# Attention: queries and keys are turned once, transfers gather each group's rows, and only the row maxima are turned in the loop

## The chip, the core and the metric

The kernel runs on one core of one Trainium2 chip. Its time is the device time of one execution in microseconds (us). The engines are TensorE (PE, with its weight loads as PEld), VectorE (DVE), ScalarE (ACT), GpSimd (POOL) and SyncE (SP), which here only issues DMAs. SBUF is the on-chip memory of 128 partitions, PSUM holds the matmul results in banks of 512 float32 per partition.

## The reference

Six layers run one after the other on 1024 tokens of width 256. The second, an attention, is what the change is about; the fifth, a state-space mixer, is touched in one place. Everything is float32.

```python
x = x + 0.5 * moe(layernorm(x))            # 8 experts, top 2
x = x + attention(layernorm(x))            # this change
x = x + 0.5 * moe(layernorm(x))
x = x + 0.5 * sparse_ffn(layernorm(x))
x = x + mamba(layernorm(x))                # one edit in its preparation
x = x + 0.5 * sparse_ffn(layernorm(x))

# attention: 32 query heads and 8 key heads of width 8
q, k = rope(x @ Wq.T), rope(x @ Wk.T);  v = x @ Wv.T
scores = einsum('bkgqd,bkld->bkgql', q, k) * 8 ** -0.5
out = einsum('bkgql,bkld->bkgqd', softmax(scores), v)
return out @ Wo.T
```

## The kernel before

The attention works through 8 groups, one per key head, with 4 query heads each. Scores are computed twice. **Chunks** (`score_chunk`, L1087) have queries on the partitions: one matmul makes 128 queries x 512 keys of one head, and VectorE takes the row maximum of each (`reduce`, L863). A group has 64 chunks, 32 for each half of its queries. Then **scoresT** (L1103) makes the same scores with keys on the partitions, this time less the row maximum, ScalarE takes the exponential (L981), and `values` (L1115) multiplies by the values; the values carry a column of ones, so that a row of the result is the softmax sum. The row maximum enters scoresT as two more rows of the contraction (a high and a low part of the maximum against two rows of -1), just as queries and keys enter in high and low parts to keep float32 accuracy.

The loop of a group has 16 **slots**: 8 key tiles for each half of the queries. In each slot TensorE runs, in an order that is written out in `body`: scoresT of heads pair 0, two chunks, scoresT of pair 1, a chunk, `values` of the slot before, a chunk. The chunks run `LEAD = HALF + 2 * PER_SLOT` = 32 + 8 = 40 chunks ahead of the exponentials, and from slot 6 on they belong to the next group. They go round three PSUM banks (`ring`): a table decides at build time which bank a job gets, and `take` makes TensorE wait until the bank's last reader is done.

Before, four more kinds of job sit in that ring. `turn_q1` (slots 3 and 4) turns the next group's stacked queries with four 128 x 128 transposes, L1063, and ScalarE copies them out (L965). `turn_q2` (slots 6 and 14) does it again with the maxima in the stack (copy L969). `turn_o` (slots 1 and 9) turns a half's output back to tokens (L1123), after which VectorE takes reciprocals of the sums (L871) and multiplies (L876) inside slots 2 and 10. The maxima go DVE `top_scores` (slots 5 and 13), POOL `split_max` (L804, L806), PE `turn_q2`, ACT `copy_q2`, PE scoresT (slots 8 and 0). GpSimd copies each group's queries and values (`copy_q`, `copy_v`). SyncE issues four transfers of 32 rows per group that put the keys into `k_picks` (L755).

Ahead of the loop there is a preparation (layer norm, projections, rotation, stacking of high and low parts, transposes) and the **lead** of 40 chunks with no exponentials beside them. Group 7 has no next group, so its slots 6 to 15 hold no chunks; there the output of the first half is turned and projected in between, the second half after the last slot.

In the mixer's preparation (`body` of `mamba_layer`'s first part) each of 8 groups has on ScalarE: first convolution tap of B (`tap(g, 0)`, L1509), SiLU of the previous group's C (L1749, L1750), `tap(g, 1)`, then `high` (L1712), the rounded part of the next group's weights. GpSimd subtracts it (L1641), and TensorE's next projection (L62) waits for that.

## Time and profile before

| | us |
|---|---|
| median of 3 runs | 1743.71 |
| lowest and highest | 1729.76, 1744.64 |
| the profiled execution | 1740.03 |
| its span, first to last instruction | 1738.2 |
| busy PE, DVE, ACT, POOL in the span | 1488.4, 1080.0, 877.6, 493.8 |
| mean granted TensorE clock, of full speed | 0.932 |

Times in the trace count from the first instruction. The attention lies from 193 to 673 us: preparation to 232.1, lead to 258.6, groups 0 to 6 to 618.3, group 7 and the end to 672.8. The mixer's preparation lies from 967 to 1069. A busy TensorE is not one at its peak: matmuls on different rows of the array overlap in the records. What bounds a stage is read from who waits for whom there, not from the busy shares of the whole.

### The profile page before, as it was taken

Reading aid. Unit: us, or ns where it says so; the run is one execution under the profiler, and the core shown is the slowest. Engines: PE = TensorE matmul, PEld = TensorE weight load, DVE = VectorE, ACT = ScalarE, POOL = GpSimd, SP = SyncE. Lnnn points to the kernel's source line nnn. Section 1 sums busy time; section 2 is a strip of 40 time slices with the busy share of each in tenths; the row PEclk is TensorE's granted clock in tenths of the full one; section 3 lists DMA queues with packets and bytes.
Section 4 is the critical chain, followed back from the end, with each engine's and each line's share of the span. In section 5 each row is a group of like instructions: output and inputs, shape, how many; then the busy total and the mean of one; then the engine's idle time right before and its main releaser. Section 6 shows DMA issues by size and latency. Waiting matters only on the chain. (4 is left out here: it accounts for less than half of the span.)

```text
span 1738.2 us, 24514 instructions
## 1 busy us (share of the span) xinstructions
PE 1488.4 (86%) x7880; PEld 1033.9 (59%) x7880; DVE 1080.0 (62%) x1948; ACT 877.6 (50%) x1268; POOL 493.8 (28%) x422
## 2 busy tenths in 40 slices
PE   3999479899998996799499787799999999999697
PEld 2566343333333334466277675688888888888586
DVE  4121577787888754212277665778777777878375
ACT  1222226676676673122143566666766666675332
POOL 1344320000000000244210112466565555565200
PEclk7999759999999997799799898999999999999799
DMA  8432210000000004623400111223232222331200
GB/s 299 122 49 40 50 25 1 13 13 12 12 12 0 12 1 153 216 43 49 104 11 1 43 34 49 88 76 100 70 99 92 73 91 73 102 93 46 76 1 25
DMA packets 78526, 107.33 MB, mean 62 GB/s; under 512 B 9600, under 2 KB 57984, under 8 KB 78432
## 3 DMA queue, kind: packets, MB, share of 16 engines
q1 hardware_dynamic: 69056, 91.98, 16.8%
q0 software_dynamic: 9376, 14.16, 4.6%
q8 instruction: 51, 0.84, 0.2%
q14 instruction: 43, 0.35, 0.1%
HBM read 89.99 MB, written 11.93 MB: 59 GB/s over the span
## 5 line engine op out<-in xcount | busy, mean ns | idle before, releaser
L981 ACT ACTIVATE attn_probs<-attn_scoresT 128x1024 f32<-128x1024 f32 x256 | 253.3, 1024 | 101.5 <-PE attn_scoresT L1103 99.0
L863 DVE TENSOR_REDUCE attn_max_chunks<-attn_scores 128x1 f32<-128x512 f32 x349 | 227.7, 685 | 48.7 <-PE attn_scores L1087 48.7
L1514 DVE SCALAR_TENSOR_TENSOR ssm_scan_x<-ssm_scan_proj,ssm_w_conv,ssm_scan_x 128x1023 f32<-128x1023 f32 (+2 forms) x96 | 123.0, 1282 | 80.8 <-ACT ssm_scan_x L1509 75.0
L1087 PE MATMUL attn_scores<-attn_k_picks,attn_qT_pass 64*128 64x512 f32 x349 | 149.8, 473 | 25.8 <-DVE attn_max_chunks L863 17.0
L1103 PE MATMUL attn_scoresT<-attn_qT_pass,attn_k_picks 64*128 64x512 f32 x512 | 163.9, 438 | 0.7 <-ACT attn_probs L981 0.7
L401 DVE TENSOR_TENSOR moe_h<-moe_silu,moe_up 128x512 f32<-128x512 f32 x46 | 31.6, 688 | 189.4 <-PE moe_up L516 189.4
L1115 PE MATMUL attn_o<-attn_probs,attn_v_group 128*32 128x512 f32 x1024 | 139.0, 615 | 0.9 <-ACT attn_probs L981 0.8
L1087 PEld LDWEIGHTS attn_scores<-attn_k_picks,attn_qT_pass 64*128 64x128 f32 x349 | 63.0, 192 | 122.6 <-DVE attn_max_chunks L863 98.2
L448 ACT ACTIVATE moe_silu<-moe_gate 128x512 f32<-128x512 f32 x46 | 27.5, 598 | 200.4 <-PE moe_gate L516 200.4
L62 PE MATMUL ssm_scan_proj<-ssm_xnT_hi,ssm_w_in_hi 128*128 128x512 f32 x256 | 108.7, 425 | 23.0 <-DVE ssm_scan_x L1514 21.0
L286 POOL DMA_INDIRECT moe_sums<-moe_y,moe_token x46 | 72.8, 1583 | 165.6 <-DVE moe_y L410 159.4
L2351 PE MATMUL ssm_scan_out<-ssm_scan_w_out,ssm_scan_v 128*128 128x256 f32 x480 | 113.5, 391 | 4.6 <-POOL ssm_scan_w_out L2056 4.4
L863 DVE TENSOR_REDUCE attn_max_chunks<-attn_turn 128x1 f32<-128x512 f32 x139 | 94.5, 680 | 28.0 <-PE attn_turn L1087 28.0
L64 PE MATMUL ssm_scan_proj<-ssm_xnT_hi,ssm_w_in_lo 128*128 128x512 f32 x256 | 102.6, 401 | 0.0
L2351 PEld LDWEIGHTS ssm_scan_out<-ssm_scan_w_out,ssm_scan_v 128*128 128x128 f32 x480 | 92.3, 197 | 17.2 <-POOL ssm_scan_w_out L2056 4.6
L63 PE MATMUL ssm_scan_proj<-ssm_xnT_lo,ssm_w_in_hi 128*128 128x512 f32 x256 | 102.3, 399 | 0.0
L804 POOL TENSOR_TENSOR attn_q_group<-attn_max,attn_zeros 128x16 fp32r<-128x16 f32 x16 | 3.6, 228 | 336.3 <-DVE attn_max L857 336.3
L2241 ACT ACTIVATE ssm_scan_gate<-ssm_scan_v 128x1024 f32<-128x1024 f32 x24 | 25.4, 1058 | 137.7 <-DVE ssm_scan_v L2134 137.7
L2034 POOL TENSOR_TENSOR ssm_scan_c_exp_cum<-ssm_cT,ssm_scan_exp_cum 128x896 f32<-128x896 f32 x32 | 70.8, 2212 | 80.9 <-PE ssm_scan_y L2325 79.5
L516 PE MATMUL moe_gate<-moe_w_gate_up,moe_xT 128*128 x184 | 90.3, 614 | 1.3 <-ACT moe_xT L442 1.3
L546 PE MATMUL moe_out<-moe_w_down,moe_hT 128*128 x368 | 87.1, 380 | 1.5 <-ACT moe_hT L454 1.5
L2042 POOL TENSOR_TENSOR ssm_scan_x_to_end<-ssm_scan_x_dt,ssm_decay_to_end 128x512 f32<-128x512 f32 x64 | 87.6, 1387 | 1.8 <-DVE ssm_scan_x_dt L2098 1.8
(337 smaller groups left out, 3415.2 us busy)
## 6 DMA issues: line engine op xcount, KB each, us to landing
ssm_cum_all<-ssm_cums SPq DMA_DIRECT2D x32, 512.0 KB, 3.8
ssm_scan_exp_cum<-ssm_cums SPq DMA_DIRECT2D x32, 512.0 KB, 3.7
moe_w_gate_up<-in_moe_w SPq DMA_DIRECT2D x16, 512.0 KB, 10.8
...
```

The source lines that it names most:

```text
L62: nc.tensor.matmul(out, lhs_hi, rhs_hi, start=start, stop=False)
L63: nc.tensor.matmul(out, lhs_hi, rhs_lo, start=False, stop=False)
L64: return nc.tensor.matmul(out, lhs_lo, rhs_hi, start=False, stop=stop)
L516: last = nc.tensor.matmul(bank[:].unsqueeze(1), xT[i % 2][:, k, :], w_in[name][:, bass.ds(e * KD + k, 1), :], start=(k == 0), stop=(k == K ...
L863: return nc.vector.tensor_reduce(rmaxc[:, half, place:place + 1], chunk_bank(g, n), AX_X, ALU.max).then_inc(reduced, 1)
L981: nc.scalar.activation(probs[s % 2][:, 2 * pair:2 * pair + 2, :], st_ps[pair][:], ACT.Exp, scale=SCALE).then_inc(exp_done, 1)
L1087: nc.tensor.matmul(chunk_bank(g, n), qm[b][head_rows(j), t * P:(t + 1) * P], kz[b][head_rows(j), j % 2, c * BANK:(c + 1) * BANK], start=Tr ...
L1103: last = nc.tensor.matmul(st_ps[pair][:, i, :], kz[b][head_rows(j), j % 2, kt * P:(kt + 1) * P], qe[b][head_rows(j), half * BANK:(half + 1 ...
L1115: last = nc.tensor.matmul(o_ps[j * STACK:(j + 1) * STACK, :], vg[b][:, kt, :], probs[s % 2][:, i, :], start=(kt == 0), stop=(kt == KT_TILE ...
L1514: return nc.vector.scalar_tensor_tensor(out[:, shift:], ps[:, :S - shift], w(k), out[:, shift:], ALU.mult, ALU.add)
L2042: nc.gpsimd.tensor_tensor(xend[:, cs, :], xdt[:, cs, :], to_end[:, cs, bass.ds(n, 1)] .broadcast_to([P, cs.stop - cs.start, PD]), ALU.mult ...
L2351: last = nc.tensor.matmul(out[:, m, :], v[:, v_row(b * NORM_HEADS + jn), cols], w_out[:, jn, :], start=(jn == 0), stop=(jn == NORM_HEADS - 1))
```

## The change

- Queries and keys are turned once, right after the rotation, by 24 transposes in place of the stacks (`turn_roped`). ScalarE rounds them (high parts), VectorE and GpSimd subtract (low parts). `roped` is no longer stacked.
- SyncE gathers each group's rows from these into `k_picks` and `q_group`: 12 transfers of 8 rows for the keys, 6 of 16 rows for the queries, and from group 2 on 2 that clear the maximum rows, 20 in all. They wait until the group before last has been read for the last time by scoresT.
- Chunks and scoresT read the same `q_group`: during the chunks its maximum rows are zero. In the loop only a 128 x 32 tile of maxima is turned, by one transpose (`turn_max`, last in slots 6 and 14); VectorE copies it out (`copy_max`, after the slot's four reductions), and two transfers put it into `q_group` (`load_max`). scoresT of slots 8 and 0 waits for their landing (`max_in`).
- Outputs are no longer turned in the loop. ScalarE still copies a half's result to SBUF; 8 transfers of 8 rows move values and sums into `o_all` and `o_sums` (`send_out`). Reciprocals, products (GpSimd) and the split for the projection come once, in group 7; only group 7's own outputs still go through transposes.
- Chunks of a half now run over all query tiles with the first 512 keys, then with the others.
- `LEAD` is not edited: 40 chunks in both kernels.
- In the mixer's preparation `high` moves ahead of the SiLU and of `tap(g, 1)`.

```diff
-        q_stack = sp.sb("q_stack", [P, TT, KV, GQ * STACK])
-        k_stack = sp.sb("k_stack", [P, TT, KV * STACK])
-        kT = sp.sb("kT", [P, 2, S], F32R)
+        qT_hi = sp.sb("qT_hi", [P, KD, S], F32R)
+        qT_lo = sp.sb("qT_lo", [P, KD, S], F32R)
+        kT_hi = sp.sb("kT_hi", [KV * HD, S], F32R)
+        kT_lo = sp.sb("kT_lo", [KV * HD, S], F32R)
+        qs = [sp.sb(f"q_group{b}", [P, S], F32R) for b in range(2)]
-        qg = [sp.sb(f"q_group{b}", [P, TT, GQ * STACK]) for b in range(2)]
-        qm = [sp.sb(f"qT_pass1_{b}", [P, S], F32R) for b in range(2)]
-        qe = [sp.sb(f"qT_pass2_{b}", [P, S], F32R) for b in range(2)]
-        oT = sp.sb("oT", [P, BANK])
+        tops = sp.sb("max_parts", [P, 2, STACK])
+        topsT = [sp.sb(f"maxT{h}", [STACK, P], F32R) for h in range(2)]
+        oT = [sp.sb(f"oT{h}", [P, BANK]) for h in range(2)]
+        o_all = sp.sb("o_all", [P, KD, S])
+        o_sum = sp.sb("o_sums", [P, KD, S])
...
         def chunk(n):
             half, r = divmod(n, HALF)
-            return TURNS[r % GQ], half * (TT // 2) + r // (2 * GQ), r // GQ % 2
+            c, r = divmod(r, HALF // 2)
+            return TURNS[r % GQ], half * (TT // 2) + r // GQ, c
...
             jobs = [("chunk", ahead, n) for ahead, n in slot_chunks(s)]
-            if s in Q1_SLOTS:
-                jobs.insert(3, ("q1", 1, Q1_SLOTS.index(s)))
-            if s == KT_TILES - 2:
-                jobs.insert(3, ("q2", 0, 1))
-            if s == SLOTS - 2:
-                jobs.insert(3, ("q2", 1, 0))
-            if s == 1:
-                jobs.insert(3, ("o", -1, 1))
-            if s == KT_TILES + 1:
-                jobs.insert(3, ("o", 0, 0))
+            if s == OWN_TOP_SLOT + 1:
+                jobs.append(("max", 0, 1))
+            if s == NEXT_TOP_SLOT + 1:
+                jobs.append(("max", 1, 0))
             return jobs
...
-            free_from[bank] = k + (3 if job[0] == "chunk" else 5)
+            free_from[bank] = k + 3
...
+            def load_k(g, src, pieces, cols, done):
+                for w in range(2):
+                    for i in range(2):
+                        for piece in pieces:
+                            at = w * SPAN + piece * PAIR_ROWS + i * HD
+                            sync.dma_start(f32(kz[g % 2][at:at + HD, i, cols]), f32(src[g * HD:(g + 1) * HD, cols])
+                                           ).then_inc(done, 16)
+            def load_group(g):
+                if g >= 2:
+                    sync.wait_ge(scoresT_done, 2 * SLOTS * (g - 1))
...
+                load_k(g, kT_hi, (0, 1), slice(0, S), kz_in[b])
+                load_k(g, kT_lo, (3,), slice(0, S), kz_in[b])
+                load_q(g, qT_hi, (0, 3), slice(0, S), q_in[b])
+                load_q(g, qT_lo, (1,), slice(0, S), q_in[b])
...
+            def load_max(g, half):
+                sync.wait_ge(m_copied, 2 * g + half + 1)
+                for w in range(2):
+                    at = w * SPAN + STACK
+                    sync.dma_start(f32(qs[g % 2][at:at + 4, half_cols(half)]),
+                                   f32(topsT[half][w * 16:(w + 1) * 16, :])).then_inc(max_in[half], 16)
+            def send_out(g, half):
+                sync.wait_ge(o_copied, 2 * g + half + 1)
+                for j in range(GQ):
+                    row = g % 4 * STACK + j * HD
+                    for dst, at in ((o_all, j * STACK), (o_sum, j * STACK + HD)):
+                        sync.dma_start(dst[row:row + HD, g // 4, half_cols(half)], oT[half][at:at + HD, :]
+                                       ).then_inc(o_out[half], 16)
...
+            load_max(0, 0)
+            for g in range(KV):
+                if g < KV - 1:
+                    load_group(g + 1)
+                if g:
+                    send_out(g - 1, 1)
+                load_max(g, 1)
+                if g < KV - 1:
+                    send_out(g, 0)
+                    load_max(g + 1, 0)
...
+            def copy_max(g, half):
+                dve.wait_ge(m_turned, 2 * g + half + 1)
...
+                nc.vector.tensor_copy(topsT[half][:], max_bank(g, half)[0:STACK, 0:P]).then_inc(m_copied, 1)
+            def reciprocals(k, half):
...
+                nc.vector.reciprocal(o_sum[rows, k, cols], o_sum[rows, k, cols]).then_inc(rec_done, 1)
...
             def scoresT(g, b, s, pair, after=None):
...
-                    pe.wait_ge(q2_done, 2 * g + half + 1)
+                    pe.wait_ge(max_in[half], 32 * (g + 1))
...
@@ mamba_layer, @block.scalar, body(g, b)
                 tap(g, 0)
+                if not last:
+                    high(g + 1, 1 - b)
                 if not first:
                     silu(g - 1, 1 - b, 1)
                 tap(g, 1)
-                if not last:
-                    high(g + 1, 1 - b)
```

TensorE, slots 6 to 8 of group 0, before (`attn_turn` is the third bank of the ring, `attn_qT_pass_1` the next group's queries):

```order
L1063 MATMUL attn_scores<-main_ident,attn_q_group 128x128 [waits attn_top_split,attn_reduced]
L1063 MATMUL attn_scores<-main_ident,attn_q_group 128x128 x3
L1087 MATMUL attn_scores<-attn_k_picks,attn_qT_pass_1 128x512 [waits attn_reduced]
L1103 MATMUL attn_scoresT<-attn_qT_pass_0,attn_k_picks 128x512 [waits attn_exp_done]
L1103 MATMUL attn_scoresT<-attn_qT_pass_0,attn_k_picks 128x512
L1087 MATMUL attn_turn<-attn_k_picks,attn_qT_pass_1 128x512 [waits attn_reduced]
L1087 MATMUL attn_scores<-attn_k_picks,attn_qT_pass_1 128x512 [waits attn_reduced]
L1103 MATMUL attn_scoresT<-attn_qT_pass_0,attn_k_picks 128x512 [waits attn_exp_done]
L1103 MATMUL attn_scoresT<-attn_qT_pass_0,attn_k_picks 128x512
L1087 MATMUL attn_scores<-attn_k_picks,attn_qT_pass_1 128x512 [waits attn_q2_done]
L1115 MATMUL attn_o<-attn_probs,attn_v_group 32x512 [waits attn_exp_done]
L1115 MATMUL attn_o<-attn_probs,attn_v_group 32x512 x3
```

and now (`attn_max_parts` is the tile of maxima, `attn_max_in1` the landing of its two transfers):

```order
L1147 MATMUL attn_scores<-attn_k_picks,attn_q_group 128x512 [waits attn_reduced]
L1127 MATMUL attn_scores<-main_ident,attn_max_parts 32x128 [waits attn_top_split,attn_reduced]
L1163 MATMUL attn_scoresT<-attn_q_group,attn_k_picks 128x512 [waits attn_exp_done]
L1163 MATMUL attn_scoresT<-attn_q_group,attn_k_picks 128x512
L1147 MATMUL attn_scores<-attn_k_picks,attn_q_group 128x512 [waits attn_reduced] x2
L1163 MATMUL attn_scoresT<-attn_q_group,attn_k_picks 128x512 [waits attn_exp_done]
L1163 MATMUL attn_scoresT<-attn_q_group,attn_k_picks 128x512
L1147 MATMUL attn_scores<-attn_k_picks,attn_q_group 128x512 [waits attn_max_copied]
L1175 MATMUL attn_o<-attn_probs,attn_v_group 32x512 [waits attn_exp_done]
L1175 MATMUL attn_o<-attn_probs,attn_v_group 32x512 x3
L1147 MATMUL attn_scores<-attn_k_picks,attn_q_group 128x512 [waits attn_reduced]
L1163 MATMUL attn_scoresT<-attn_q_group,attn_k_picks 128x512 [waits attn_exp_done,attn_max_in1]
```

Four transposes ahead of a slot's last chunk have become one behind it, and the wait of the first scoresT of slot 8 is no longer for a copy of ScalarE but for a transfer.

SyncE, one group in the loop, now (before, it held two rows, `attn_k_picks<-attn_kT 32x1024`, four transfers, behind the same wait):

```order
L749 DMA attn_k_picks<-attn_kT_hi 8x1024 [waits attn_scoresT_done]
L749 DMA attn_k_picks<-attn_kT_hi 8x1024 x7
L749 DMA attn_k_picks<-attn_kT_lo 8x1024 x4
L757 DMA attn_q_group<-attn_qT_hi 16x1024 x4
L757 DMA attn_q_group<-attn_qT_lo 16x1024 x2
L774 DMA attn_q_group<-attn_no_max 4x1024 x2
L788 DMA attn_o_all<-attn_oT 8x512 [waits attn_o_copied]
```

Seven more of `attn_o_all` and `attn_o_sums` follow, then the two of `attn_maxT`, then the same ten for the other half. All 40 stand in one queue in this order.

## Rows read from the trace of the kernel before

**Rows 1.** Windows of core 0: its four attention stages; busy per engine, TensorE clock, DMA.
```profile
232.10:258.60 26.50, 22.12 (x44) 10.64 (x44) 22.99 (x39) 1.87 (x2) 1.56 (x3) 0.50 0.07 16
258.60:618.30 359.70, 325.96 (x1949) 127.88 (x1948) 288.60 (x489) 245.68 (x265) 15.12 (x40) 0.98 0.04 9
```

**Rows 2.** Timeline, all engines, one plain slot; start, duration, engine, then idle before.
```profile
452.71 0.50 PE L1087 MATMUL attn_turn<-attn_k_picks,attn_qT_pass 64*128 64x512 f32 x1
...
453.25 0.69 DVE L863 TENSOR_REDUCE attn_max_chunks<-attn_turn 128x1 f32<-128x512 f32 x1 [0.22 <-PE attn_turn L1087]
...
454.00 0.50 PE L1087 MATMUL attn_turn<-attn_k_picks,attn_qT_pass 64*128 64x512 f32 x1
...
454.43 1.07 PE L1115 MATMUL attn_o<-attn_probs,attn_v_group 128*32 128x512 f32 x8
...
455.42 0.49 PE L1087 MATMUL attn_scores<-attn_k_picks,attn_qT_pass 64*128 64x512 f32 x1
```

**Rows 3.** Timeline of ACT over one group of heads.
```profile
414.68 1.94 ACT L981 ACTIVATE attn_probs<-attn_scoresT 128x1024 f32<-128x1024 f32 x2 [1.08 <-PE attn_scoresT L1103]
...
417.30 1.94 ACT L981 ACTIVATE attn_probs<-attn_scoresT 128x1024 f32<-128x1024 f32 x2
420.59 1.02 ACT L981 ACTIVATE attn_probs<-attn_scoresT 128x1024 f32<-128x1024 f32 x1 [1.35 <-PE attn_scoresT L1103]
...
427.18 1.03 ACT L981 ACTIVATE attn_probs<-attn_scoresT 128x1024 f32<-128x1024 f32 x1
...
446.56 1.02 ACT L981 ACTIVATE attn_probs<-attn_scoresT 128x1024 f32<-128x1024 f32 x1 [1.35 <-PE attn_scoresT L1103]
...
450.78 1.94 ACT L981 ACTIVATE attn_probs<-attn_scoresT 128x1024 f32<-128x1024 f32 x2 [1.90 <-PE attn_scoresT L1103]
453.48 1.94 ACT L981 ACTIVATE attn_probs<-attn_scoresT 128x1024 f32<-128x1024 f32 x2 [0.76 <-PE attn_scoresT L1103]
...
465.55 1.02 ACT L981 ACTIVATE attn_probs<-attn_scoresT 128x1024 f32<-128x1024 f32 x1 [1.08 <-PE attn_scoresT L1103]
```

**Rows 4.** Timeline of SyncE, first eight key transfers of the attention.
```profile
227.77 5.03 SPq L755 DMA_DIRECT2D attn_k_picks<-attn_kT  x8
```

**Rows 5.** Instructions of tile attn_k_picks: its last line.
```profile
DMA to landing us min/median/max: 2.3/2.4/3.5
```

**Rows 6.** DMA issues by line: an 8 KB transfer; KB each, us to landing.
```profile
moe_w_gate<-in_moe_gate SPq DMA_DIRECT2D x2, 8.0 KB, 1.7
```

**Rows 7.** Timeline of SyncE, start of the next layer: a 512 KB load.
```profile
676.69 1.23 SPq L258 DMA_DIRECT2D moe_w_up<-in_moe_w  x1
```

**Rows 8.** Groups by form on DVE: count, busy us, mean ns, idle before.
```profile
L2115 DVE COPY ssm_scan_states<-ssm_scan_turn 128x128 f32<-128x128 f32 x32 | 9.0, 282 | 1.7 <-PE ssm_scan_turn L2317 1.7
...
L871 DVE RECIPROCAL attn_recip<-attn_scores 128x16 f32<-128x16 f32 x15 | 3.7, 249 | 8.0 <-PE attn_scores L1123 8.0
...
L316 DVE RECIPROCAL moe_rstd<-moe_std 128x4 f32<-128x4 f32 x4 | 0.7, 178 | 2.3 <-ACT moe_std L427 2.3
```

**Rows 9.** Groups by form on POOL, a 512-element subtraction.
```profile
L765 POOL TENSOR_TENSOR attn_w_o_lo<-attn_w_o,attn_w_o_hi 128x512 fp32r<-128x512 f32 x1 | 1.3, 1270 | 2.0 <-ACT attn_w_o_hi L1011 2.0
```

**Rows 10.** Windows: a stretch of the loop at the lower clock.
```profile
396.00:400.00 4.00, 3.69 (x15) 1.41 (x16) 1.27 (x4) 0.61 (x1) 0.00 (x0) 0.57 0.00 0
```

**Rows 11.** Timeline, all engines, the lead before the loop.
```profile
232.11 1.22 PE L1087 MATMUL attn_scoresT<-attn_k_picks,attn_qT_pass 64*128 64x512 f32 x4 [1.40 <-DMA attn_k_picks<-attn_kT]
...
236.53 2.48 DVE L863 TENSOR_REDUCE attn_max_chunks<-attn_scoresT 128x1 f32<-128x512 f32 x4
```

**Rows 12.** Timeline, all engines, one group of the second mixer's preparation.
```profile
1019.16 1.27 POOL L1641 TENSOR_TENSOR ssm_prep_w_bc_lo<-ssm_prep_w_bc,ssm_prep_w_bc_hi 128x512 fp32r<-128x512 f32 x1 [8.75 <-ACT ssm_prep_w_bc_hi L1712]
...
1020.57 0.50 PE L62 MATMUL ssm_prep_proj<-ssm_xnT_hi,ssm_prep_w_bc_hi 128*128 128x512 f32 x1 [1.60 <-POOL ssm_prep_w_bc_lo L1641]
...
1025.27 6.75 DVE L1514 SCALAR_TENSOR_TENSOR ssm_prep_conv<-ssm_prep_proj,ssm_w_conv,ssm_prep_conv 128x1023 f32<-128x1023 f32 x5 [1.82 <-ACT ssm_prep_conv L1509]
...
1029.18 1.27 POOL L1641 TENSOR_TENSOR ssm_prep_w_bc_lo<-ssm_prep_w_bc,ssm_prep_w_bc_hi 128x512 fp32r<-128x512 f32 x1 [8.74 <-ACT ssm_prep_w_bc_hi L1712]
```

513 lines of the change are left out of this document (275 added, 238 removed).

## The prediction

> **What bounds the kernel now.** I read the windows by stage first, to see how much of the execution the change can reach: 26.5 us of lead and 359.7 us of loop over groups 0 to 6, a fifth of the span [rows 1]. In the loop no engine is full: TensorE 326 of 360 us, VectorE 289, ScalarE 246. So the loop is bound by a round of waits, and the timeline of one plain slot shows it [rows 2]. The slot's last chunk starts on TensorE at 452.71, its reduction at 453.25. When that ends at 453.94, the bank is free and the third chunk of the next slot starts at 454.00. `values` follows at 454.43, and only behind it, at 455.42, the next last chunk. The round takes 2.71 us, whatever else fits beside it.
>
> ScalarE's timeline gives the length of every slot of a group, as the distance between its first exponentials [rows 3]: slot 0 takes 2.62 us, slot 1 3.29, slots 2 and 3 together 6.59, slots 4 to 9 19.38, slot 10 4.22, slot 11 2.70, slots 12 to 15 12.07. That is 50.87 for a group. Sixteen plain slots would be 43.2, so 7.7 us per group are paid for the jobs that turn queries, maxima and outputs, and for the reciprocal and the product in slots 2 and 10.
>
> **The loop, groups 0 to 6.** The turns of queries (8 transposes per group), of outputs (8) and of the old stack with maxima (8) go, with ScalarE's four copies and VectorE's reciprocals and products. With them goes the irregular use of the three banks, where such a job held one for five places. What stays is 43.2 us of plain slots, the copies of the output (slots 0 and 8), which already fit in a slot of 2.62, and the new way of the maxima. I count from T, the moment the last chunk of slot 6 starts.
> - `turn_max` comes right behind it, one small transpose instead of four. It is done by about T + 0.3, and I cost it at nothing because it is over before anything that the round waits for: the third chunk starts only when the reduction is, 1.29 us after the last chunk [rows 2].
> - VectorE finishes the last reduction at T + 1.2 and copies the maxima. The nearest row is a PSUM copy of 128 x 128 at 282 ns [rows 8]; the columns are as many, so I take 0.25, which makes T + 1.5. The third chunk of slot 7 now waits for this copy instead of the reduction, so slot 7 is longer by 0.25 and one more handover, 0.43 in all.
> - SyncE issues two transfers. It issues one each 0.63 us (eight in 5.03, [rows 4]); the second starts at about T + 2.1. Landing: 1.7 us for 8 KB from HBM [rows 6], 2.3 to 3.5 for 128 KB from SBUF to SBUF [rows 5]. It is 8 KB from SBUF, so I take 2.0: landed and seen at T + 4.2.
> - scoresT of slot 8 could start at T + 3.1. It stands 1.1 us, with all chunks queued behind it. Of that 0.4 is absorbed, because from scoresT to the third chunk a slot has slack (1.29 us from 452.71 to 454.00, where some 0.9 would do). The round shifts by 0.7.
>
> This happens twice per group (slots 7 and 8, slots 15 and 0): 2 x (0.43 + 0.7) = 2.3, and a group takes 45.5 us. Bounds: with a landing of 1.7 the stand shrinks to 0.4 and the group takes 44.9; with 3.5 it is 48.5.
>
> Seven groups at 45.5 are 318.5. The 359.7 of today hold 7 x 50.87 = 356.1 and 3.6 more: a slow first slot, and two places where the granted clock falls to its lower level, 1.2 GHz, after TensorE had stood idle in slot 10; one is a stretch of 4.0 us at 0.57 of full speed [rows 10], which costs up to 4.0 x 0.43 = 1.7 us. I keep 4.5 for such places, since there will be other stands. New loop 323.0: **-36.7 us**.
>
> The cover of all this is SyncE's queue, which now issues 40 transfers per group instead of four. 40 x 0.63 is 25 of 45.5 us, but the order counts. The 20 of `load_group` can start about 0.4 us before slot 0 does, are issued by 12.3 and landed by 14.6; they are needed at slot 6, at about 17. Eight of `send_out` follow and end at 17.3; `load_max` is wanted at about 21. So nothing is late, with 2.4 and 4 us to spare.
>
> **The lead.** Rotation gets cheaper (no stacking beside it), but 18 transfers must be issued before the first chunk, where 4 were, and 18 more beside the first 16 chunks. The first transfers can start some 10 us before today's 227.8 [rows 4], since half of the keys go as soon as tile 3 is turned; 18 x 0.63 + 2 = 13 us later the first chunk starts, at 230 to 232, against 232.11 [rows 11]. The second half's keys land about 11 us later, when 16 chunks at 0.62 (four reductions in 2.48 us, [rows 11]) are through. The lead ends with two transfers instead of one copy. **0**, between -3 and +4.
>
> **Group 7 and the end.** Slots 1 to 3 lose their excess (1.2 us) and ScalarE two copies of 0.6. Against it: the stand at slot 8, here 1.1 in full, because ScalarE sets the pace. And VectorE gets four reciprocals of 512 elements. By the rows, 16 elements take 249 ns and 4 take 178 [rows 8], 5.9 ns per element, so 3.1 us each; the other end is 0.7, the time of a reduction of 512 [rows 2]. At 3.1 two of them, with GpSimd's products at 1.27 [rows 9] between, keep VectorE from `last_outputs` until some 4.5 us after TensorE wants to turn them. The other two end before the last slot. Together **+3.2**, between -2 and +7.
>
> **The mixer's preparation.** Today TensorE waits 1.60 us for GpSimd's low part in each group [rows 12], five times alike, with a period of 10.02 (1019.16 to 1029.18). With `high` moved up, the low part is ready over 3 us earlier. What ends last then is VectorE: it starts its taps 4.70 us after the projection (1020.57 to 1025.27), three take 3 x 6.75 / 5 = 4.1, so the period becomes 8.8 to 8.9. **-5.7**, between 0 and -8 (the whole wait).
>
> **Sum.** -36.7 + 0 + 3.2 - 5.7 = -39.2 against the profiled execution's own 1740.0 (span 1738.2 and 1.8 around it): 1700.8. The median of the three runs is 3.7 above the profiled one; I put half of that on top and say **1702**.
>
> **Rivals.**
> - *SyncE's queue is late* (slower). For: the issue of one transfer lasts 1.23 us when the queue backs up [rows 7], and nothing shows transfers of 8 rows, which may drain worse than those of 32. Against: eight in a row at 0.63 without growing [rows 4]. With an issue of c us the 20 loads are late by 20 c + 2.4 - 0.4 - 17 at slot 6, from c = 0.75 on, and `load_max`, eight transfers later, by 8 c - 6.6 more: 28 c - 21.6 per group. The gain is eaten at c near 0.97; at 1.2 that is 12.0 seven times, in all **1785**. The Trainium skill (DMA: Bandwidth & Descriptors, section Bandwidth) says to batch transfers to 1 MiB or more and that those under 64 KB are dominated by their descriptors. By that rule the change, which cuts four of 128 KB into 40 of 64 KB and less, goes the way of this rival; the trace does not bear it out, as far as 128 KB reach. Chance 0.08.
> - *Slow landing.* Each landing is at the 3.5 end, since two transfers write four partitions each. A group takes 48.5, the sum is 21 less: **1722**. For: a maximum of 3.5 was seen [rows 5]. Against: the median is 2.4. Chance 0.13.
> - *The clock.* TensorE's stands at slots 8 and 0 bring the lower level as slot 10 does in two of seven groups today. At 1.7 us each, fourteen are 19 more than the 4.5 I kept: **1720**. Against: the new stands are no longer than the one in slot 10. Chance 0.07.
> - *It doesn't do what it says.* Its last clause, 40 chunks ahead instead of 44, is not in the code; the distance is 40 in both. That costs and gains nothing. A slip in the use of banks, so that plain slots grow by 0.3 us, would leave a group at 50.3 and the whole at **1736**. Chance 0.06.
>
> My own case, 1690 to 1716 by the bounds of its terms, has the remaining 0.66. The range of **1688 to 1727** takes it in with the second and third rival and leaves out about 0.17. A measurement of this kernel tells a change from none at about 1%, 17 us: **faster 0.86, same 0.06, slower 0.08**.
>
> **What would show it.** ScalarE's slots: 14 of 16 at 2.7 us, slot 7 near 3.1, slot 8 with a wait of TensorE on the maxima's transfer of about 1 us; group period 45.5. SyncE: 0.6 us per transfer, loads done before slot 6. VectorE: reciprocals of 3 us in group 7, ScalarE standing near slot 10. Preparation: period 8.9, no wait for the low part. It is wrong if TensorE waits for `kz_in` or `q_in` in slot 6, if landings pass 3 us, or if plain slots are not 2.7.

## The result and the profile after

The changed kernel takes 1692.43 us (median of 4 runs, 1691.81 to 1694.71), the kernel before in the same session 1739.3 (4 runs, 1729.76 to 1744.64): a ratio of 0.9739, 95% interval 0.9689 to 0.9789. It is faster by 2.6%. The forecast was 1702 with a range of 1688 to 1727. The profiled execution took 1694.71 (span 1692.9), 45.3 us less than before's 1740.03, where the forecast had 39.2 less.

Where the 45.3 us came from, by stage, in us. A stage begins with its first weight transfer or, in the attention, with the first exponential of a group, which is 1.2 us later than the cuts of the windows in [rows 1]:

| stage | before | after | difference | forecast |
|---|---|---|---|---|
| first layer | 193.0 | 195.6 | +2.6 | 0 |
| attention, preparation and lead | 66.9 | 65.9 | -1.0 | 0 |
| groups 0 to 6 | 359.6 | 317.7 | **-41.9** | -36.7 |
| group 7 and the end | 55.7 | 62.2 | **+6.5** | +3.2 |
| second MoE, sparse layer | 286.4 | 282.1 | -4.3 | 0 |
| mixer's preparation, to `ssm_cums` | 70.25 | 64.12 | **-6.1** | -5.7 |
| all behind it | 706.4 | 705.3 | -1.1 | 0 |

The lines with a forecast of 0 hold nothing that was edited (but for the lead); in the twelve kernels of this study, where these layers are the same, the first layer took 191.9 to 195.6 us and the second MoE 181.7 to 185.3. So their -2.8 in sum is not to be put down to the change.

Windows of the changed kernel: lead, groups 0 to 6, group 7 with the end. Columns as in [rows 1].

```profile
core 0: us, PE busy (x) PEld busy (x) DVE busy (x) ACT busy (x) POOL busy (x), PEclk, DMA share, GB/s
232.00:261.50 29.50, 21.01 (x45) 10.42 (x47) 25.65 (x44) 0.00 (x0) 0.45 (x2) 0.50 0.09 17
261.50:579.20 317.70, 300.91 (x1800) 115.31 (x1800) 285.19 (x476) 222.44 (x238) 8.66 (x34) 0.99 0.15 24
579.20:641.40 62.20, 48.48 (x287) 22.11 (x283) 37.87 (x52) 33.28 (x37) 10.61 (x10) 0.88 0.02 3
```

TensorE is now busy 301 of 318 us in the loop, where it was 326 of 360 [rows 1], and its clock is 0.99. In the last window it is 0.88, where it was 1.00 before (618.3 to 672.8): there the clock fell, in two places.

ScalarE's timeline over one group, the one that answers to [rows 3]:

```profile
353.40 1.94 ACT L1059 ACTIVATE attn_probs<-attn_scoresT 128x1024 f32<-128x1024 f32 x2 [1.73 <-PE attn_scoresT L1163]
...
366.48 1.94 ACT L1059 ACTIVATE attn_probs<-attn_scoresT 128x1024 f32<-128x1024 f32 x2 [0.77 <-PE attn_scoresT L1163]
369.18 1.94 ACT L1059 ACTIVATE attn_probs<-attn_scoresT 128x1024 f32<-128x1024 f32 x2 [0.76 <-PE attn_scoresT L1163]
372.31 2.16 ACT L1059 ACTIVATE attn_probs<-attn_scoresT 128x1024 f32<-128x1024 f32 x2 [1.19 <-PE attn_scoresT L1163]
376.15 1.94 ACT L1059 ACTIVATE attn_probs<-attn_scoresT 128x1024 f32<-128x1024 f32 x2 [1.67 <-PE attn_scoresT L1163]
...
378.50 1.94 ACT L1059 ACTIVATE attn_probs<-attn_scoresT 128x1024 f32<-128x1024 f32 x2
...
395.12 1.94 ACT L1059 ACTIVATE attn_probs<-attn_scoresT 128x1024 f32<-128x1024 f32 x2 [1.17 <-PE attn_scoresT L1163]
398.80 1.02 ACT L1059 ACTIVATE attn_probs<-attn_scoresT 128x1024 f32<-128x1024 f32 x1 [1.74 <-PE attn_scoresT L1163]
```

Slot 0 takes 2.29 and slot 8 2.35, ten slots 2.70 (366.48 to 369.18 is one), slots 6 and 14 3.13 and 3.11, slots 7 and 15 3.84 and 3.68 (slot 7 is 3.55 to 3.64 in the other groups). This group has 45.40, groups 3 to 6 have 45.09, 45.21, 45.11 and 44.98. A slot here ends with the first exponential of the next, so TensorE's stand ahead of its slot 8 shows in slot 7: the long slots are the forecast's two pairs, named by ScalarE one earlier.

The chain of the maxima, all engines, in the same group:

```profile
371.12 0.50 PE L1147 MATMUL attn_scores<-attn_k_picks,attn_q_group 64*128 64x512 f32 x1
...
371.57 0.28 PE L1127 MATMUL attn_scores<-main_ident,attn_max_parts 128*32 128x128 f32 x1
...
372.55 0.27 DVE L924 CAST attn_maxT<-attn_scores 32x128 fp32r<-32x128 f32 x1
...
372.85 1.36 SPq L780 DMA_DIRECT2D attn_q_group<-attn_maxT  x2
...
375.61 0.50 PE L1163 MATMUL attn_scoresT<-attn_q_group,attn_k_picks 64*128 64x512 f32 x2 [0.77 <-DMA attn_q_group<-attn_maxT]
```

`turn_max` follows the last chunk (371.12) by 0.45 and is no hindrance. The copy starts at 372.55, 1.43 behind the chunk, and takes 0.27 (forecast 1.2 and 0.25). Two issues take 1.36. The second began at about 373.5 and TensorE goes on at 375.61: **2.1 us from issue to use**, 2.0 in the forecast. The wait is 0.77 us of idle time behind the last chunk.

SyncE, the 20 loads of a group that starts at 398.80:

```profile
396.86 5.35 SPq L749 DMA_DIRECT2D attn_k_picks<-attn_kT_hi  x8
...
408.67 1.28 SPq L774 DMA_DIRECT2D attn_q_group<-attn_no_max  x2
```

20 transfers in 13.1 us, 0.66 each whether they carry 16, 32 or 64 KB. The last issue lasts from 10.5 to 11.2 us after slot 0; with the 2.1 us from above it has landed at 12.6. TensorE asks in slot 6, at 15.4. Nothing waits for them.

VectorE by form, the new reciprocals beside those of [rows 8]:

```profile
L929 DVE RECIPROCAL attn_o_sums<-attn_o_sums 128x512 f32<-128x512 f32 x2 | 6.7, 3342 | 0.0
```

A reciprocal of 512 elements takes 3.34 us (forecast 3.1), almost five reductions of the same width.

Group 7, where the forecast was too low. VectorE, GpSimd, TensorE and ScalarE around slot 10:

```profile
596.98 6.54 DVE L929 RECIPROCAL attn_o_sums<-attn_o_sums 128x512 f32<-128x512 f32 x2
...
605.13 1.27 POOL L875 TENSOR_TENSOR attn_o_all<-attn_o_all,attn_o_sums 96x512 f32<-96x512 f32 x1
606.44 0.42 DVE L934 CAST attn_xnT_hi<-attn_o_all 96x512 fp32r<-96x512 f32 x1 [2.63 <-POOL attn_o_all L875]
606.78 0.25 DVE L940 RECIPROCAL attn_recip<-attn_scores 128x16 f32<-128x16 f32 x1
...
607.41 0.66 PE L1195 MATMUL attn_scores<-main_ident,attn_xn 128*128 128x128 f32 x4 [1.23 <-DVE attn_xn L943]
608.10 0.58 ACT L1064 CAST attn_xnT_hi<-attn_scores 32x512 fp32r<-32x512 f32 x1 [3.54 <-PE attn_scores L1195]
608.70 3.85 ACT L1059 ACTIVATE attn_probs<-attn_scoresT 128x1024 f32<-128x1024 f32 x4
...
613.66 0.41 PE L63 MATMUL attn_scores<-attn_w_o_lo,attn_xnT_hi 128*128 128x256 f32 x1
...
616.98 3.77 ACT L1059 ACTIVATE attn_probs<-attn_scoresT 128x1024 f32<-128x1024 f32 x4 [4.42 <-PE attn_scoresT L1163]
```

The two reciprocals end at 603.5. VectorE's next instruction but one is the high part of GpSimd's second product, which ends at 606.4, and only then come the few hundred ns of `last_outputs` (606.78) for which TensorE's `turn_final` waits (607.41), for which ScalarE's `last_high` waits (608.10), behind which the exponentials of slot 10 stand (608.70). The slot takes 6.11 us. TensorE did 0.66 us of work between 606.2 and 609.8, and from 610 to 616 its clock is at 1.2 GHz: the projection's matmuls take 0.41 us, in `e5` below, where there is no such stand, 0.28. That makes a second long slot of 6.45 (4.94 in the profile of `e1`, which has the same code here).

The stage's 6.5 us are thus not one loss. From the first exponential of slot 0 to that of slot 15, group 7 takes 45.2 us where it took 41.15: 4.1 more. The other 2.5 lie behind the last slot (17.0 us, 14.5 before), where the second half is projected, and there too the clock was low:

```profile
632.00:636.00 4.00, 4.00 (x20) 4.00 (x20) 0.69 (x1) 0.00 (x0) 0.00 (x0) 0.50 0.00 0
```

The stands ahead of this projection are nearly the same in both kernels (0.71 and 0.68 us, then 1.06 before and 1.55 after), and with the same code the stretch took 14.7 us in the profile of `e3` and 16.2 in those of `e1` and `e6`. What decides whether the clock falls there isn't shown.

The mixer's preparation, GpSimd's subtraction that answers to [rows 12]:

```profile
984.88 1.29 POOL L1704 TENSOR_TENSOR ssm_prep_w_bc_lo<-ssm_prep_w_bc,ssm_prep_w_bc_hi 128x512 fp32r<-128x512 f32 x1 [7.62 <-ACT ssm_prep_w_bc_hi L1775]
993.77 1.29 POOL L1704 TENSOR_TENSOR ssm_prep_w_bc_lo<-ssm_prep_w_bc,ssm_prep_w_bc_hi 128x512 fp32r<-128x512 f32 x1 [7.59 <-ACT ssm_prep_w_bc_hi L1775]
```

The period is 8.89, forecast 8.8 to 8.9; it was 10.02.

### The profile page after: what moved, and what is told of

Read it like the earlier page. It is cut to its first block and busy times, and to the rows that moved or that the text cites. A ratio compares the mean times of both kernels' runs of the same rounds, so it can differ in the third digit from the quotient of the medians.

```text
span 1692.9 us, 24339 instructions
## 1 busy us (share of the span) xinstructions
PE 1461.9 (86%) x7712; PEld 1021.0 (60%) x7712; DVE 1088.5 (64%) x1946; ACT 844.6 (50%) x1206; POOL 491.1 (29%) x409
## 5 line engine op out<-in xcount | busy, mean ns | idle before, releaser
L918 DVE TENSOR_REDUCE attn_max_chunks<-attn_scores 128x1 f32<-128x512 f32 x488 | 306.4, 684 | 35.1 <-PE attn_scores L1147 34.5
L1059 ACT ACTIVATE attn_probs<-attn_scoresT 128x1024 f32<-128x1024 f32 x256 | 248.3, 1023 | 138.9 <-PE attn_scoresT L1163 138.8
L1147 PE MATMUL attn_scores<-attn_k_picks,attn_q_group 64*128 64x512 f32 x488 | 184.3, 460 | 8.2 <-DVE attn_max_chunks L918 1.9
L1147 PEld LDWEIGHTS attn_scores<-attn_k_picks,attn_q_group 64*128 64x128 f32 x488 | 84.5, 190 | 165.1 <-DVE attn_max_chunks L918 158.6
L1163 PE MATMUL attn_scoresT<-attn_q_group,attn_k_picks 64*128 64x512 f32 x512 | 150.5, 442 | 17.3 <-DMA attn_q_group<-attn_maxT 14.2
L2097 POOL TENSOR_TENSOR ssm_scan_c_exp_cum<-ssm_cT,ssm_scan_exp_cum 128x896 f32<-128x896 f32 x32 | 70.6, 2206 | 82.4 <-PE ssm_scan_y L2388 81.5
L845 POOL TENSOR_TENSOR attn_max_parts<-attn_max,attn_zeros 128x16 fp32r<-128x16 f32 x16 | 3.6, 223 | 312.0 <-DVE attn_max L913 312.0
L1163 PEld LDWEIGHTS attn_scoresT<-attn_q_group,attn_k_picks 64*128 64x128 f32 x512 | 75.0, 188 | 31.3 <-issue 13.4
L516 PE MATMUL moe_up<-moe_w_up,moe_xT 128*128 x184 | 88.1, 602 | 0.0
## 6 DMA issues: line engine op xcount, KB each, us to landing
moe_w_gate_up<-in_moe_w SPq DMA_DIRECT2D x16, 512.0 KB, 11.2
```

Source lines behind the costliest of these rows:

```text
L516: last = nc.tensor.matmul(bank[:].unsqueeze(1), xT[i % 2][:, k, :], w_in[name][:, bass.ds(e * KD + k, 1), :], start=(k == 0), stop=(k == K ...
L918: return nc.vector.tensor_reduce(rmaxc[:, half, place:place + 1], chunk_bank(g, n), AX_X, ALU.max).then_inc(reduced, 1)
L1059: nc.scalar.activation(probs[s % 2][:, 2 * pair:2 * pair + 2, :], st_ps[pair][:], ACT.Exp, scale=SCALE).then_inc(exp_done, 1)
L1147: nc.tensor.matmul(chunk_bank(g, n), qs[b][head_rows(j), t * P:(t + 1) * P], kz[b][head_rows(j), j % 2, c * BANK:(c + 1) * BANK], start=Tr ...
L1163: last = nc.tensor.matmul(st_ps[pair][:, i, :], kz[b][head_rows(j), j % 2, kt * P:(kt + 1) * P], qs[b][head_rows(j), half_cols(half)], sta ...
```

## The experiments

Each was timed beside the kernel before, whose median was 1739.3 to 1740.6 in these sessions. The stages are those of one profile each. All in us:

| kernel | median | ratio to before | groups 0 to 6 | a middle group | group 7, end | mixer's prep. |
|---|---|---|---|---|---|---|
| before | 1739.7 | 1 | 359.6 | 50.87 | 55.7 | 70.3 |
| after | 1692.43 | 0.9739 (0.9689, 0.9789) | 317.7 | 45.1 | 62.2 | 64.1 |
| e1 | 1700.47 | 0.9775 (0.9745, 0.9805) | 317.5 | 45.1 | 59.8 | 72.1 |
| e2 | 1690.90 | 0.9728 (0.9703, 0.9753) | 317.5 | 45.1 | 59.0 | 66.2 |
| e3 | 1684.25 | 0.9689 (0.9662, 0.9717) | 309.2 | 43.8 | 58.7 | 66.0 |
| e4 | 1682.34 | 0.9682 (0.9657, 0.9707) | 307.4 | 43.7 | 56.3 | 64.1 |
| e5 | 1688.19 | 0.9717 (0.9695, 0.9740) | 317.6 | 45.1 | 53.6 | 66.0 |
| e6 | 1740.67 | 1.0012 (0.9996, 1.0027) | 366.1 | 51.4 to 54.2 | 59.8 | 64.1 |
| e7 | 1719.13 | 0.9890 (0.9868, 0.9912) | 336.7 | 48.0 | 54.5 | 72.9 |
| e8 | 1672.49 | 0.9633 (0.9613, 0.9654) | 306.8 | 43.7 | 54.4 | 64.1 |
| e9 | 1704.76 | 0.9765 (0.9723, 0.9808) | 333.9 | 47.4 | 54.2 | 65.9 |
| e10 | 1706.85 | 0.9801 (0.9768, 0.9833) | 337.6 | 48.1 | 53.8 | 65.3 |

The same code differs by up to 2.7 us in the last column and by 2.4 in the one before it (after and e1), so single differences of that size say nothing by their sum; where one matters, a line of the trace is shown.

**e1, the mixer's edit undone.**

```diff
                 tap(g, 0)
-                if not last:
-                    high(g + 1, 1 - b)
                 if not first:
                     silu(g - 1, 1 - b, 1)
                 tap(g, 1)
+                if not last:
+                    high(g + 1, 1 - b)
```

> The changed kernel with `high` put back behind the SiLU and tap(g, 1) in the mixer's preparation; nothing else. My theory: TensorE's wait for GpSimd's low part (1.6 us per group) is what `high` moved up takes away, so the stretch from the preparation's first load to the first transfer of `ssm_cums` goes back from 64.1 to about 70 us (before: 70.25), the period of a group from 8.8 to 10.0, and the time from 1692.4 to 1698. The attention stays as it is (loop 317.6). Rival: the 6.1 us there come from something else than this edit (the clock, or other data in the cache of instructions); then the stretch stays at 64 to 65 and the time at 1692.

GpSimd's subtractions are 10.02 apart again:

```profile
982.27 1.27 POOL L1704 TENSOR_TENSOR ssm_prep_w_bc_lo<-ssm_prep_w_bc,ssm_prep_w_bc_hi 128x512 fp32r<-128x512 f32 x1 [8.74 <-ACT ssm_prep_w_bc_hi L1775]
992.29 1.27 POOL L1704 TENSOR_TENSOR ssm_prep_w_bc_lo<-ssm_prep_w_bc,ssm_prep_w_bc_hi 128x512 fp32r<-128x512 f32 x1 [8.74 <-ACT ssm_prep_w_bc_hi L1775]
```

From the first of the eight subtractions to the last it takes 79.8 us in the kernel before, 71.3 in the changed one, 81.5 in e1. The edit is worth 4 to 9 us in this stage (with `high` moved up it took 64.1 to 66.2 in the profiles above, without 70.3 to 72.9), in a settled period 1.13. The attention has no part in it: its loop takes 317.5 in e1 and 317.7 in the changed kernel.

**e2 and e5, two orders in group 7.** e2 is the first hunk, e5 both.

```diff
                     high_parts(0, 0)
-                    high_parts(1, 0)
                 if s == KT_TILES + 1:
                     last_outputs(0)
+                    high_parts(1, 0)
...
-                    if last and s == KT_TILES + 1:
+                    if last and s == KT_TILES + 2:
                         last_high(0)
```

> The changed kernel with one edit in group 7: VectorE does last_outputs(0) ahead of high_parts(1, 0), which waits for GpSimd's second product. My theory: the 6.11 us slot (9 to 10) is long because last_outputs stands behind that product (done 606.4), not because of the reciprocals as such (done 603.5). last_outputs then runs at about 605 and not 606.8, the slot falls from 6.11 to about 3.5, TensorE keeps its full clock, so that the projection of slot 11 takes 1.6 instead of 2.9 us and its slot falls from 6.45 to about 4. Group 7 is 4 to 6 us shorter, time 1687 to 1689. Rival: the reciprocals alone hold VectorE and with it the turns; then the slot falls by under 1.5 us, the lower clock stays, and the time is 1691. Second rival: the projection of slot 11 now waits for the low part that comes later; then slot 11 takes what slot 9 gives, 1692.

> The kernel of e2 (VectorE's last_outputs ahead of high_parts(1, 0)) with ScalarE's last_high(0) moved behind the exponentials of slot 10 as well. In e2 ScalarE stands at last_high (603.8) ahead of the exponentials of slot 10, and what it waits for, turn_final, comes on TensorE only in slot 10, behind scoresT and `values`. My theory: this order, not the reciprocals, makes the rest of the long slot; slot 9 to 10 falls from 4.83 to about 2.5, the clock stays at its full level, and the slot with the projection (11 to 12) falls from 5.33 to about 3.5. Group 7 with the end goes from 59.0 to 55.5 us, time 1687. Rival: the projection then waits for VectorE's last_low or GpSimd's low part, and slot 11 takes the gain: 58 to 59 us, 1690.

e2: the slot fell from 6.11 to 4.83 only and the one of the projection to 5.33; the clock still fell. These are the numbers of the first rival, but not its cause, for the reciprocals no longer hold anything: `last_outputs` follows TensorE's turn of the outputs at once. It is ScalarE that waits, in `last_high`, for the other turn:

```profile
601.54 0.26 DVE L940 RECIPROCAL attn_recip<-attn_scores 128x16 f32<-128x16 f32 x1 [0.76 <-PE attn_scores L1186]
...
603.81 0.58 ACT L1064 CAST attn_xnT_hi<-attn_scores 32x512 fp32r<-32x512 f32 x1 [2.26 <-PE attn_scores L1195]
```

e5: the slot is 2.40, the next one 2.57, that of the projection 3.10. ScalarE's timeline in e5:

```profile
602.22 1.98 ACT L1059 ACTIVATE attn_probs<-attn_scoresT 128x1024 f32<-128x1024 f32 x2
604.62 1.94 ACT L1059 ACTIVATE attn_probs<-attn_scoresT 128x1024 f32<-128x1024 f32 x2 [0.43 <-PE attn_scoresT L1163]
606.59 0.58 ACT L1064 CAST attn_xnT_hi<-attn_scores 32x512 fp32r<-32x512 f32 x1
607.19 1.94 ACT L1059 ACTIVATE attn_probs<-attn_scoresT 128x1024 f32<-128x1024 f32 x2
610.29 3.77 ACT L1059 ACTIVATE attn_probs<-attn_scoresT 128x1024 f32<-128x1024 f32 x4 [1.16 <-PE attn_scoresT L1163]
```

`last_high` now costs its 0.58 us between two pairs of exponentials. All four reciprocals are still there. So what slots 0 to 15 lost was not the reciprocals' own time but two instructions that stood ahead of work they had nothing to do with. From the first exponential of slot 0 to that of slot 15 it takes 43.7 to 45.2 us with the old orders (after, e1, e3, e6), 42.8 in e2 and 38.9 in e5. With both moved group 7 is 2.1 us shorter than before; in e5 the clock did not fall behind the last slot either (14.7 us), in e8, with the same two orders, it did (17.0), so that part is not the orders' doing. ScalarE's move alone was not run.

**e3 and e4, two ways to take away the stand at slots 8 and 0.**

```diff
# e3
-                jobs.append(("max", 0, 1))
+                jobs.insert(3, ("max", 0, 1))
-                jobs.append(("max", 1, 0))
+                jobs.insert(3, ("max", 1, 0))
# e4
-LEAD = HALF + 2 * PER_SLOT
+LEAD = HALF + 3 * PER_SLOT
```

> The changed kernel with turn_max and copy_max ahead of the slot's last chunk (slots 6 and 14), not behind it. My theory: the stand at slots 8 and 0 is the tail of the chain turn, copy, two issues, landing. The copy comes 0.5 us earlier (one reduction ahead), so TensorE's wait for the maxima's transfer falls from 0.77 to about 0.3 us and a group from 45.2 to 44.5; loop 317.6 to 313, time 1687 to 1689. Rival: the turn delays the last chunk by its 0.28 us and the round through that chunk's reduction hands this on, so that a group stays at 45.2 and the time at 1692.

> The changed kernel with LEAD = HALF + 3 * PER_SLOT: 44 chunks ahead in place of 40. The maxima are turned in slots 5 and 13, a slot earlier; the next group's chunks begin in slot 5. My theory: the maxima's transfers then land before slot 8 and 0 ask for them, so no slot stands: a group goes from 45.2 to 43.7 or 44.3. Against it stands the loads' deadline: they are issued by 11.2 us after a group's start and land at about 13.2, and slot 5 starts at 13.5 to 14, so they are just in time. The lead grows by four chunks, 2.5 us. In group 7 the reciprocals start a slot earlier, so the slot 9 to 10 of 6.11 us shrinks by 2 to 3. Sum: -7 to -10 in the loop, +2.5, -2 to -5: 1682 to 1687. Rival: the loads are late at slot 5 in each group by 1 to 2 us; then the loop gains nothing, and the time is 1692 to 1700, which would be the reason for 40.

Both hold, e3 with more than expected. Of e4's smaller terms two missed: preparation and lead grew by 1.1 us and not 2.5, and the long slot of group 7 shrank by 0.9 (to 5.24) and not by 2 to 3. In e3 the copy starts 2.8 us after its slot's first exponential instead of 3.4, and the stand is:

```profile
369.41 0.50 PE L1163 MATMUL attn_scoresT<-attn_q_group,attn_k_picks 64*128 64x512 f32 x2 [0.24 <-DMA attn_q_group<-attn_maxT]
```

0.24 us where it was 0.77, and a group loses 1.3 us. In e4 no scoresT of the loop waits for the maxima, a group takes 43.7, and the loads, issued in time for slot 5, make no slot longer. The stand is thus worth 1.4 us per group, three quarters of the 1.9 by which a group of the changed kernel exceeds sixteen plain slots. A slot more of distance for the maxima is a slot less for the loads, and they can just spare it: SyncE's last issue begins 10.1 us after a group's start, and slot 5 asks at 13.0.

**e6, the suspected price of SyncE's queue doubled.**

```diff
-                            sync.dma_start(f32(kz[g % 2][at:at + HD, i, cols]), ...
+                            for c in ((half_cols(0), half_cols(1)) if cols == slice(0, S) else (cols,)):
+                                sync.dma_start(f32(kz[g % 2][at:at + HD, i, c]), ...
```

> The changed kernel with each of a group's 12 key transfers in the loop split in two halves of 512 columns (24 transfers, the same bytes): the suspected price of SyncE's queue doubled where it is covered. My theory: an issue costs 0.62 to 0.67 us whatever it carries, so the loads are issued by 18.7 and not 11.2 us after a group's start and land at about 20.5; slot 6 asks at 16.6. TensorE then waits some 4 us in slot 6 for kz_in and q_in and a group takes 49 to 50 us in place of 45.2: the loop 344 to 350, time 1719 to 1725. Rival: an issue costs by its bytes; then 24 halves take about as long as 12, nothing is late, and the time is 1692 to 1695. Second rival: the engines of the DMA, not the issues, set the landing; then issues stay at 0.63 but landings pass 3 us.

SyncE and TensorE in one group of e6 (start 361.81):

```profile
360.50 10.97 SPq L750 DMA_DIRECT2D attn_k_picks<-attn_kT_hi  x15
371.52 5.29 SPq L750 DMA_DIRECT2D attn_k_picks<-attn_kT_lo  x8
...
380.65 1.27 SPq L775 DMA_DIRECT2D attn_q_group<-attn_no_max  x2
```

```profile
376.83 0.72 PE L1164 MATMUL attn_scoresT<-attn_q_group,attn_k_picks 64*128 64x512 f32 x2
383.57 0.87 PE L1148 MATMUL attn_scores<-attn_k_picks,attn_q_group 64*128 64x512 f32 x2 [6.02 <-DMA attn_q_group<-attn_no_max]
```

```profile
383.50:388.00 4.50, 4.43 (x15) 1.49 (x15) 2.05 (x4) 1.02 (x1) 0.00 (x0) 0.50 0.14 24
```

The columns of the last row are those of the windows above. Half the bytes cost the same issue: 23 key transfers in 16.3 us, 0.71 each. TensorE stands 6.02 us for the last of the 32 and goes on at half its clock (0.50). Direction and cause are those of my theory, the size is not: the loop grew by 48.4 us, where I expected 26 to 32. An issue with the gap behind it is 0.71 and not 0.62, slot 6 asks a good microsecond earlier than I wrote, and after the stand the clock stays at its lower level for nearly 10 us, so that a group loses 1.4 to 3.0 us more than its stand (5.1 to 6.0). The landing is not late, 2.3 us from the last issue to TensorE's next chunk: the second rival is out. **Twelve more small transfers per group eat the whole gain**: 1740.67 against 1739.7.

**e7, the kernel before without the turns of the next group's queries.** It reads group 0's queries in all chunks, and the exponential's scale is 0.

```diff
-            if s in Q1_SLOTS:
-                jobs.insert(3, ("q1", 1, Q1_SLOTS.index(s)))
...
-                    if s in Q1_SLOTS and not last:
-                        copy_q1(g + 1, 1 - b, Q1_SLOTS.index(s))
...
-                nc.tensor.matmul(chunk_bank(g, n), qm[b][head_rows(j), t * P:(t + 1) * P],
+                nc.tensor.matmul(chunk_bank(g, n), qm[0][head_rows(j), t * P:(t + 1) * P],
```

> The kernel before with the two turns of the next group's queries (turn_q1 with its copy, slots 3 and 4) left out in the loop: all groups' chunks read group 0's queries; the exponential's scale is 0 so that nothing overflows. It computes other numbers, with the same instructions otherwise. My theory: the 7.7 us over plain slots are paid by the six jobs that sit in the ring for five places, 1.3 us each, so a group goes from 50.9 to about 48.3 and the loop from 359.6 to 341; time 1721. Rival: the excess lies in the jobs of slots 10 and 14 (outputs and maxima with their waits), and the queries' turns hide in the slack of their slots; then the loop gives at most 0.6 us a group, and the time is 1735 to 1739.

A group goes from 50.87 to 48.0, 2.87 for two jobs. ScalarE in e7, slots 0 to 3:

```profile
404.66 1.94 ACT L979 ACTIVATE attn_probs<-attn_scoresT 128x1024 f32<-128x1024 f32 x2 [1.08 <-PE attn_scoresT L1100]
...
407.28 1.94 ACT L979 ACTIVATE attn_probs<-attn_scoresT 128x1024 f32<-128x1024 f32 x2
410.57 1.02 ACT L979 ACTIVATE attn_probs<-attn_scoresT 128x1024 f32<-128x1024 f32 x1 [1.35 <-PE attn_scoresT L1100]
...
413.89 1.94 ACT L979 ACTIVATE attn_probs<-attn_scoresT 128x1024 f32<-128x1024 f32 x2 [1.01 <-PE attn_scoresT L1100]
```

Slot 1 with its job and slot 2 behind it take 3.29 and 3.32. Each of the four jobs that are left lengthens two slots, its own and the next, by 0.59 to 0.68. In slot 2 TensorE waits 0.55 us for a reduction: one of the three banks still holds the turned outputs then. So two jobs less should give 2.4 us. The rest lies in slot 10, which took 4.22 before and takes 3.29 in e7, less 0.36 that slot 7 grew. The table of banks is another one with two jobs fewer; in the kernel before, slot 10's third chunk had got the bank of the turned outputs and waited for VectorE's product:

```profile
448.58 0.50 PE L1087 MATMUL attn_scores<-attn_k_picks,attn_qT_pass 64*128 64x512 f32 x1 [0.77 <-DVE attn_xn L876]
```

So the rival, which looked to slot 10, has a part too. The run takes transposes, copies and banks away together; that the held bank, and not the copies, makes the slots long is read from these waits, it is not isolated. Groups 1 to 6 all take 47.9 to 48.0, while before two of seven were 1.4 longer, by a fall of the clock.

**e8, e3, e4 and e5 together.** The diff is theirs.

> The changed kernel with all of it: 44 chunks ahead, maxima turned and copied ahead of a slot's last chunk, VectorE's last_outputs ahead of high_parts(1, 0), ScalarE's last_high(0) behind the exponentials of slot 10. My theory: with 44 chunks no slot stands for the maxima, so the earlier copy adds little: a group 43.4 to 43.8 (43.7 in e4), loop 306; the two orders in group 7 give what they give in e5: group 7 and the end 53 to 54. Sum against e4 (loop 307.4, end 56.3): -1 and -3, time 1677 to 1680. Rival: the turn ahead of the last chunk costs its 0.28 us where there is no stand to take away, and a group grows to 44.2: 1681.

1672.49 us (1672.25 to 1677.31): 20 below the changed kernel, 67 below before. In the loop the parts add up: e3 adds 0.6 us, since behind 44 chunks there is no stand left. Group 7 gained 1.9 and not 3, because of the low clock behind the last slot. The time is even so 4.5 us below the expected range. The profiled executions of e4 and e8 lie 5.7 apart, of which 2.5 are in the second MoE, which nobody edited; the medians lie 9.9 apart, and where the rest of that is isn't shown.

**e9 and e10, `values` moved in a plain slot.** Both have 44 chunks and the orders of e5.

```diff
# e9: both chunks ahead of values
-                    jobs(1)
+                    jobs(2)
# e10: none
-                    jobs(1)
```

> The changed kernel with 44 chunks ahead and the two orders of group 7 (as in e8), the maxima again last in their slots, and on TensorE a slot's fourth chunk ahead of `values`, not behind it. It puts the round to the test that I took as the bound of a plain slot: last chunk, its reduction, the next slot's third chunk, `values`, the next last chunk, 2.71 us. My theory: with `values` out of that round nothing of 2.71 us is left, and VectorE's four reductions (0.60 us from one to the next) or TensorE's own work (2.5 us of a slot) end last; a plain slot falls to 2.45 to 2.6 and the loop from 306.8 to 280 to 296, time 1650 to 1665. Rival: TensorE is full in a plain slot, as its 94 to 95 us busy of 100 say, and the order changes nothing: slots 2.70, time 1673. Second rival: the fourth chunk now waits for the first one's bank ahead of `values`, which then is late: slots 2.9, time 1695.

> The same with `values` ahead of the third and the fourth chunk. My theory of the round: the third chunk waits for the reduction of the last one as before, and `values` stands ahead of both, so the round holds last chunk, reduction, third chunk, last chunk: shorter than 2.7 too, but `values` of the slot before now comes at the moment its exponentials end, so TensorE waits for ScalarE up to 0.4 us; a plain slot 2.5 to 2.7, time 1655 to 1673. Rival: TensorE is full, 2.70, time 1673.

Both are slower than e8 by 32 to 34 us, with plain slots of 2.93 in both. In e9 it is the second rival: the fourth chunk waits for the first one's bank in every slot. In e10 my own theory fails, and the rival too. There the second chunk waits, for the reduction of the third chunk of the slot before, which now comes late, behind `values`. The waits of e9 and e10:

```profile
419.11 0.49 PE L1147 MATMUL attn_scores<-attn_k_picks,attn_q_group 64*128 64x512 f32 x1 [0.32 <-DVE attn_max_chunks L918]
```

```profile
416.50 0.49 PE L1147 MATMUL attn_scores<-attn_k_picks,attn_q_group 64*128 64x512 f32 x1 [0.32 <-DVE attn_max_chunks L918]
```

Plain slots alone, two of the kernel before, five of the changed one, three each of e9 and e10:

```profile
453.48:458.88 5.40, 5.22 (x34) 2.02 (x32) 4.97 (x9) 3.88 (x4) 0.00 (x0) 1.00 0.00 0
```

```profile
378.50:392.01 13.51, 13.16 (x82) 5.15 (x81) 12.43 (x21) 9.69 (x11) 0.00 (x0) 1.00 0.05 10
```

```profile
412.26:421.06 8.80, 7.84 (x50) 3.03 (x48) 7.63 (x13) 5.82 (x6) 0.00 (x0) 1.00 0.37 61
```

```profile
410.13:418.92 8.79, 7.83 (x49) 2.80 (x48) 7.45 (x13) 6.15 (x6) 0.00 (x0) 1.00 0.39 63
```

Per slot TensorE is busy 2.61, 2.63, 2.61 and 2.61 us, and idle 0.09, 0.07, 0.32 and 0.32. The work is the same in all four; the two orders lose by the one wait of 0.32.

## Why the prediction was right, point by point

- **The loop, forecast 323.0, measured 317.7.** Sixteen plain slots of 2.70 and twice a longer slot pair is what the trace shows: 45.1 per group, forecast 45.5. The slot with the copy is longer by 0.42 (forecast 0.43), the landing 2.1 (2.0). The stand adds 0.9 to the next slot, and the one behind it gives 0.37 back; that is 0.5, where I had 0.7. With that a group is 0.4 shorter than forecast. The rest was the 4.5 us kept for slow places: 2.0 are left, 1.6 of them in group 0. The landing that counts took 2.1 us, so the rival of the slow landing fails. In e7 too the falls of the clock went when two turns went, and the new stands bring none: the rival of the clock fails in the loop.
- **What the turns cost.** Of the excess of 7.7 us a group keeps 1.9, which are the new way of the maxima. e7 bears out that two jobs less give 2.9. I had it as "irregular use of the banks", and the waits fit that: two slots of 0.59 for each job, and 0.9 in slot 10 for a chunk that the table put on a bank still in use.
- **SyncE's queue.** Forecast 0.63 per transfer, measured 0.66; the loads have 2.8 us to spare (15.4 less 12.6), forecast 2.4. That this fits is partly luck: they land 2.0 us earlier than forecast, and are needed 1.6 earlier. e6 bears out the rival's mechanism, with the number of transfers in place of their price. The rule of the Trainium skill that was set against this change (DMA: Bandwidth & Descriptors, section Bandwidth: transfers of 1 MiB or more, and under 64 KB the descriptors dominate) is half borne out. Here a small transfer costs SyncE 0.66 us with 8 KB and with 64 KB alike, so small ones do pay by their number. But where nobody waits for them no cost is seen: plain slots are 2.70 with many transfers running (slots 1 to 5, DMA share 0.34) and with few (9 to 13, 0.05).
- **Preparation and lead: 0 forecast, -1.0 measured**, inside its bounds. The first chunk came 2.0 us earlier in the stage, the lead is 1.1 longer, for it ends with 2.1 us of waiting for the maxima's transfer.
- **Group 7: +3.2 forecast, +6.5 measured**; this term was mis-sized, near its upper bound. A reciprocal was priced well (3.34, forecast 3.1; 5.9 ns per element make 3.2, not 3.1), its effect was not: `last_outputs` came 2.3 us after TensorE's turn and not 4.5. What was missing: ScalarE stands in `last_high` too, for a turn that TensorE does only in its slot 10, and behind the two stands (1.23 and 1.72 us) the clock was low from 610 to 616, so that the projection's slot grew as well. Slots 0 to 15 took 4.1 us more than before. The other 2.5 are the low clock behind the last slot, for which the forecast had no term. I had written "the other two end before the last slot" and looked at no other engine's order. e2 alone did not mend it, e5 did.
- **The mixer: -5.7 forecast, -6.1 by the stage.** The period came out at 8.89. e1 ties it to the one edit.
- **What bounds a plain slot.** I named a round of waits and said that no engine is full. For plain slots that was wrong: TensorE was busy 5.22 of 5.40 us there already in the kernel before. The window's 326 of 360 us was a mean over plain slots and long ones. The round is there, but no order with the same matmuls side by side could have given more than 0.07 to 0.09 us a slot; e9 and e10, which broke it up, only added a wait. Whether TensorE could do this work in less, with more matmuls side by side, isn't shown. The sum did not rest on it, since it took 2.70 as measured.

The terms missed by -5.2, +3.3, -1.0 and -0.4 us, and -2.8 lay in layers that were not touched. So the profiled execution is 6.1 below its sum, and without the opposite miss in group 7 it would be more. The median is 9.6 below the forecast, since I put 1.2 on top and the profiled execution is 2.3 above the median.
